# Masked products and states in wider vector instructions, and one subtraction issued a slot later, in a linear-attention pipeline

## What is computed

```python
qkv = x @ Wqkv.T + bqkv
q = (jax.nn.elu(q) + 1.0 + FEAT_EPS) / jnp.sqrt(E)
k = jax.nn.elu(k) + 1.0 + FEAT_EPS
kv_cumsum = jnp.cumsum(jnp.einsum('blhe,blhf->blhef', k, v), axis=1)
num = jnp.einsum('blhe,blhef->blhf', q, kv_cumsum)
den = jnp.einsum('blhe,blhe->blh', q, jnp.cumsum(k, axis=1))[..., None] + FEAT_EPS
out = (num / den).reshape(B, L, D)
```

## Time and profile before

| what | value |
|---|---|
| median of 3 runs | 722.83 us (722.69 to 724.22) |
| span of the profiled execution, first to last instruction | 705.1 us |
| its own total | the profile gives the span alone |
| busy PE, DVE, ACT, POOL | 629.5, 609.4, 494.0, 418.5 us |
| mean granted TensorE clock | 0.970 of full speed |
| first masked product, last masked product start | 31.0, 231.2 us |

### The profile page before, as it was taken

How to read it: one execution, slowest core, us unless ns; L and a number is a source line. 1 busy time by engine, 2 the same in 40 slices (tenths; PEclk the granted TensorE clock), 3 DMA queues, 4 the chain that set the end, 5 groups by cost and what they waited for, 6 DMA issues and landing times.

```text
span 705.1 us, 16639 instructions
## 1 busy us (share of the span) xinstructions
PE 629.5 (89%) x5448; PEld 323.9 (46%) x5448; DVE 609.4 (86%) x1566; ACT 494.0 (70%) x1007; POOL 418.5 (59%) x931
## 2 busy tenths in 40 slices
PE   4599689889887798899999999999999999899994
PEld 2366566666555322222323323233333322498994
DVE  6878999998977898899999999999999995686552
ACT  3634656766645347888888888888898889855662
POOL 6212666575656457135676787887777872566553
PEclk9899999999999959999999999999999999999997
DMA  6664133243263313016430120302103001456600
GB/s 180 176 215 122 49 111 108 97 158 106 92 203 98 89 46 110 26 54 202 121 91 2 58 69 13 113 25 87 39 19 109 25 12 35 138 171 175 173 31 12
DMA packets 42900, 66.26 MB, mean 94 GB/s; under 512 B 7948, under 2 KB 36335, under 8 KB 39808
## 3 DMA queue, kind: packets, MB, share of 16 engines
q1 hardware_dynamic: 39232, 56.73, 26.8%
q0 software_dynamic: 3296, 8.41, 3.3%
q10 hardware_dynamic: 288, 0.07, 0.0%
HBM read 41.64 MB, written 22.26 MB: 91 GB/s over the span
## 4 chain that ended last, share of the span: by engine, by line
PE 51%; DVE 20%; ACT 17%; issue 6%; POOL 3%; DMA 1%; SPq 1%; ACTq 0%; POOLq 0%; DVEq 0%
PE bank L1081 11%; ACT arena L2000 10%; PE pair L1070 7%; DVE arena L1569 6%; PE bank L1042 6%; PE pair L1331 4%; DVE arena L1402 4%; PE pair L1340 2%; PE bank L1340 2%; DVE arena L1431 2%; PE bank L1092 2%; PE bank L936 2%; ACT arena L1969 2%; PE bank L925 2%; DVE arena L1552 1%
## 5 line engine op out<-in xcount | busy, mean ns | idle before, releaser
L2000 ACT ACTIVATE arena<-pair 128x512 f32<-128x512 f32 x506 | 278.1, 602 | 50.5 <-PE pair L1070 48.6
L1569 DVE TENSOR_REDUCE arena<-bank 128x1 f32<-128x512 f32 x388 | 251.3, 682 | 7.5 <-PE bank L1042 6.5
L1070 PE MATMUL pair<-q_stack,k_stack 64*128 64x512 bf16 x506 | 158.0, 386 | 5.9 <-ACT arena L2000 5.3
L1042 PE MATMUL bank<-k_stack,q_stack 63*128 63x512 bf16 x388 | 137.4, 395 | 8.6 <-DVE arena L1569 4.8
L1081 PE MATMUL bank<-arena,values 128*9 128x512 f32 x1024 | 134.7, 598 | 1.6 <-ACT arena L2000 1.5
L1402 DVE TENSOR_TENSOR arena<-bank,cst 128x512 f32<-128x512 f32 x128 | 82.1, 682 | 15.6 <-PE bank L910 15.1
L1569 DVE TENSOR_REDUCE arena<-pair 128x1 f32<-128x512 f32 x124 | 84.3, 680 | 1.5 <-PE pair L1042 1.1
L1042 PEld LDWEIGHTS bank<-k_stack,q_stack 63*128 63x128 bf16 x388 | 33.3, 93 | 109.6 <-DVE arena L1569 24.9
L715 POOL TENSOR_TENSOR arena<-arena 128x32 f32<-128x32 f32 (+6 forms) x312 | 68.8, 220 | 24.4
L1070 PEld LDWEIGHTS pair<-q_stack,k_stack 64*128 64x128 bf16 x506 | 40.6, 93 | 48.6 <-ACT arena L2000 26.4
L1914 ACT ACTIVATE arena<-bank,den_eps 128x512 f32<-128x512 f32 x32 | 21.7, 677 | 41.2 <-PE bank L936 41.2
(11 more groups left out here) (301 smaller groups left out, 1262.0 us busy)
## 6 DMA issues: line engine op xcount, KB each, us to landing
softmax_parts<-arena SPq DMA_DIRECT2D x8, 768.0 KB
q_stack<-softmax_parts SPq DMA_DIRECT2D x48, 128.0 KB, 2.9
k_stack<-softmax_parts SPq DMA_DIRECT2D x48, 128.0 KB, 3.0
linear_parts<-arena SPq DMA_DIRECT2D x7, 768.0 KB, 3.7
q_stack<-linear_parts SPq DMA_DIRECT2D x42, 128.0 KB, 2.9
k_stack<-linear_parts SPq DMA_DIRECT2D x42, 128.0 KB, 2.9
arena<-in_L_ffn_w_dram SPq DMA_DIRECT2D x16, 256.0 KB, 4.5
v_all<-token_rows SPq DMA_DIRECT2D x20, 192.5 KB, 2.7
```

Of the source, the lines that this page charges most:

```text
L1042: pe.matmul(bank[:], qs[b % 2][rows, slot, qt * P:(qt + 1) * P], ks[b % 2][rows, slot, :], start=True, stop=True).then_inc(d_s_m, 1)
L1070: pe.matmul(score_bank(s)[:], ks[u][rows, 2 * g + x, kt * P:(kt + 1) * P], qs[u][rows, 2 * g + x, :], start=True, stop=True).then_inc(d_s_ ...
L1569: dve.reduce_max(mx[:, m % 2, col:col + 1], bank[:], AX).then_inc(d_s_mr, 1)
L2000: act.activation(pt[:, kt % 2, x, half, :], score_bank(s)[:], ACT.Exp, scale=SCALE).then_inc(d_s_e, 1)
```

## The change

Three edits on DVE, with the counts of the signals in the lists that wait for them. The two banks of the products become one PSUM tensor of 1,024 columns, `low`, with `bank[0]` and `bank[1]` as its halves, and `masked` takes them in one instruction with one signal. `state_masked` does three states in one instruction, by a pattern of four dimensions. `a_rest(s + 2, 0)` goes from slot 6 to slot 7, right before `a_rest(s + 2, 1)`.

```diff
@@ -83,7 +83,9 @@
-        k.bank = [top.enter_context(nc.psum_tensor(f"bank{i}", [P, 4 * P], F32)) for i in range(4)]
+        k.low = top.enter_context(nc.psum_tensor("low", [P, 8 * P], F32))
+        k.bank = [k.low[:, 0:512], k.low[:, 512:1024]]
+        k.bank += [top.enter_context(nc.psum_tensor(f"bank{i}", [P, 4 * P], F32)) for i in range(2, 4)]
         k.pair = [top.enter_context(nc.psum_tensor(f"pair{i}", [P, 8 * P], F32)) for i in range(2)]
@@ -902,7 +904,7 @@ products(g)
-                    wait(pe, s_am, 2 * g)
+                    wait(pe, s_am, g)
@@ -929,7 +931,7 @@ numerators(g)
-                    pe.wait_ge(s_am, 2 * g + 2)
+                    pe.wait_ge(s_am, g + 1)
@@ -1130,7 +1132,7 @@ early_maximum(m)
                     if m == 0:
-                        pe.wait_ge(s_am, 2 * B * NL)
+                        pe.wait_ge(s_am, B * NL)
@@ -1398,18 +1400,15 @@
                 def masked(g):
                     dve.wait_ge(s_at, g + 1)
                     wait(dve, s_nm, g - 1)
-                    for gg in range(2):
-                        dve.tensor_tensor(b_am[:, g % 2, gg], k.tiles(b_at[gg][:], GH), k.rep(k.causal, GH),
-                                          ALU.mult).then_inc(s_am, 1)
+                    dve.tensor_tensor(b_am[:, g % 2].rearrange("p u j q -> p (u j) q"), k.tiles(k.low[:], 2 * GH),
+                                      k.rep(k.causal, 2 * GH), ALU.mult).then_inc(s_am, 1)
 
                 def state_masked(b):
                     dve.wait_ge(s_sm, b + 1)
-                    w = H * (E + 1)
-                    for c in range(C - 1):
-                        last = dve.tensor_tensor(spad[b % 2][:, c, :].rearrange("p (h w) -> p h w", h=H)[:, :, 0:E + 1],
-                                                 b_z[:, c * w:(c + 1) * w].rearrange("p (h w) -> p h w", h=H),
-                                                 k.hmask.unsqueeze(2).to_broadcast([P, H, E + 1]), ALU.mult)
-                    last.then_inc(s_sp, 1)
+                    states = spad[b % 2].rearrange("p c (h w) -> p c h w", h=H)[:, :, :, 0:E + 1]
+                    sums = b_z[:, 0:(C - 1) * H * (E + 1)].rearrange("p (c h w) -> p c h w", c=C - 1, h=H)
+                    dve.tensor_tensor(states, sums, k.hmask.unsqueeze(1).unsqueeze(3).to_broadcast([P, C - 1, H, E + 1]),
+                                      ALU.mult).then_inc(s_sp, 1)
@@ -1794,8 +1793,8 @@
                             a_feature(s + 2, 1)
                             if s == -1:
                                 masked(0)
+                        if d == 7 and has(s + 2):
                             a_rest(s + 2, 0)
-                        if d == 7 and has(s + 2):
                             a_rest(s + 2, 1)
```

## The result

The changed kernel takes 729.33 us (median of 10 runs, 723.61 to 730.12), the kernel before, run beside it, 722.70 us (10 runs, 721.38 to 724.22). The ratio is 1.008, with a 95% interval of 1.0065 to 1.0095: 6.6 us slower where +1.6 was forecast, and above the range.

The account below looks back on a forecast made before the run. No single engine was named as bound; the chain of waits through the batch pipeline was costed alone. Terms 0.13 - 0.14 + 1.80 - 0.05 + 1.1 - 1.08 - 0.2 gave about +1.6 us, 724.4 us, range 721.0 to 726.8.

Parts of the forecast that it names:

- step 0 to 1: Pipeline transition without a stall to win: ScalarE's second part 1.80 us later, all on the chain; two masks save 0.14.
- Step 1 to 2: Pipeline transition: ScalarE 0.77 us late, but PE's next products wait for masked(1)'s end; nearly nothing, -0.05 us.
- Step 2 to 3: Pipeline transition: the port stall becomes a stall on ScalarE's queue, +0.37 us, likewise in the two transitions after it.
- The part behind step 5: Pipeline's end: masked(0) no longer waits for the stalled subtraction, -1.08 us; three merges on the chain, -0.2 us.
- what would show it: Trace signs: subtraction 0.68 us eight times, longer ScalarE wait, c_rest idle, masked(1) waiting over 2 us, DVE's busy time falling.
- The wide mask: Masked products on DVE: one instruction over 1,024 columns lasts 1.214 us and saves 0.067 us per pair.
- the 19 pieces: Pieces in a row on PE, without a gap, after its turn at 56.85 us; part of the chain delayed by 1.80 us.
- The time around the span: Part of the run outside the profiled span, taken as 17.7 us and left unchanged.
- A: The forecast, in the pipeline: ScalarE's wait replaces the port stall, 724.4 us; chance 0.47.
- B: Rival, at c_rest of slot 0: the next step does not wait for ScalarE, DVE's gain counts, -5.9, 717 us; chance 0.15.
- C: Rival, masked products: access over both banks costs another start, 1.9 us more than the forecast, 726.3 us; chance 0.15.
- D: Rival: each wide mask saves 0.15 us, or ScalarE's delay in s = 0 is partly taken up; 723.4 us; chance 0.23.

Follow-up runs that it names:

- e10: Changed kernel plus transposes nobody reads on PE, ahead of its real wait in slot 0 of steps 1 to 5; 710.73 us, ratio 1.0041 to before.
- e2: Kernel before with only the subtraction moved to slot 7, products and states masked as before; 714.6 us, ratio 1.0074.
- e7: Kernel before with only ScalarE's second part of q put behind the next slot's numerator copy, subtraction left in slot 6; 707.98 us, ratio 1.0002.
- e9: Changed kernel unaltered, timed on the third chip against the kernel before; 714.01 us, ratio 1.006.
- e1: Kernel before, no edit, run again to see its common profile; 708.85 us, ratio 1.0002.
- e6: Kernel before with the subtraction moved and ScalarE's second part of q behind the next numerator copy, without the merges; 704.59 us, ratio 0.9954.
- e3: Kernel before with only the two merges of masks, the subtraction left in its old slot; 708.2 us, ratio 0.9999.
- e4: Changed kernel with, from slot 7 of step 0 on, ScalarE's second part of q behind the next slot's numerator copy; 705.0 us, ratio 0.9955.

## Why the prediction was right or wrong

**The sum without the clock was right.** In e10, in steps with no star, against before: step 0 to 1 is 23.90 - 22.25 = +1.65 us, forecast 1.80 - 0.14 = +1.66. Step 1 to 2 is -0.19, forecast -0.05. Step 2 to 3 is +0.38, forecast +0.37; the changed kernel itself has +0.39, and +0.37 in step 4 to 5. The part behind step 5 is -1.27, though with a star, forecast -1.08 - 0.2. The signs of "what would show it" are in the trace, all but one: 0.68 us eight times, ScalarE's longer wait (1.96), c_rest's idle released by L1983, masked(1) waiting 2.73 us in s = 1, and no step shorter that was to be longer. The one is DVE's busy time, 8.6 us lower where 9 at least was forecast. The wide mask was forecast a little short, 1.214 for 1.224 us, since the time for a column was taken from two different kinds of instruction.

**The failed step is the one from 0 to 1**, and with it the -0.05 of step 1 to 2: "on which PE's turn, the products and masked(1) at 57.85 hang. +1.80, all on the chain". I shifted the 19 pieces behind PE's turn as a rigid block, with the durations of the trace of before. I worked out that the block would start late, but never that PE would stand idle longer for it, 2.80 instead of 0.80 us, and so never asked what the clock would do: the sum has no term for matmuls that run slower behind the wait, which is to say that it put them at nothing without a reason. The missing term, changed against before less the forecast: 3.11 - 1.66 = 1.45 us in step 0 to 1, 1.27 + 0.05 = 1.32 in step 1 to 2, 1.17 - 0.37 = 0.80 in step 3 to 4, 0.58 behind step 5, and 0.31 ahead of the first relu, which e2, e7, e9 and e10 have as well as the unaltered kernel of e1 (46.94) and which is no effect of the change. These are the remainders, step by step, of the 4.5 us between +6.05 and the forecast +1.57 at the row maximum, and not yet a price of the clock, as the execution shown of before is a fast one. Against e1, whose row maximum is at 236.99, that of e9 is 4.5 us later, and 2.9 are left above the forecast; between the medians 5.5 - 1.6 = 3.9 us are.

That the added idle brings on the added slow stretches is shown by e10, which took away a part of the idle in front of PE's turns and left ScalarE's order and the time of PE's turn as they were: 3.3 us of the 5.5 us of e9 went. That is the size of the missing term as far as it was measured; e10 leaves some of the idle and two slow stretches in place. What it leaves, 710.73 - 708.47 = 2.3 us, is near the forecast +1.6. The count of idle times above points the same way, six stretches behind six waits of 2.80 us and more, and none behind the 1.40 and 1.39 us that e10 leaves. So do single executions of e9: the mean granted clock was 0.967 to 0.968 in four of them, which took 708.9 to 711.2 us, and 0.956 to 0.962 in eight, at 713.8 to 715.4. The four are near the forecast, before's 708.47 + 1.6.

**The time around the span** was wrong too, but cancels: the sum was made on a difference.

**The rivals.** A was the mechanism, mis-sized by the clock. B stated rightly what DVE's gain is worth, and by what it is decided: with ScalarE's second part out of the way (e6), the steps with a stall are 26.59 - 25.53 = 1.06 us shorter each, for the stall's 1.09. C fell with e3. Of D, the merges shorten an undisturbed step by 0.10 us in e4 against e6 and by 0.24 in e3 against before, where I had counted one merge at 0.067; e3's time shows no gain clear of its interval.

**Still open.** Why an idle time of 1.5 to 2.1 us is followed by a slow stretch in one place and not in another, which makes the stretches of the kernel before (one in the shown execution, three in e1, partly at other places in e7), and so why one execution has a star where another of the same kernel has none. The executions of e9 at 709 us were not traced, so it is not shown that they lack the stretches behind the long waits. Whether a shorter filling would do, and whether filling the 2.1 us ahead of 223 us, which e10 left alone, would take away the last one, was not tried.

## What to carry to other kernels

When a wait moves from one engine to another, work out how long TensorE stands idle in the new order and not only when it starts again: here 2 us more idle cost 1.7 us by the delay and about 1.5 by slower matmuls behind it (step 0 to 1 of e9 against e10). An instruction moved later on one engine needs its reader moved on the other: the move alone lost 6 us, the order alone gave nothing, both together gained 3.3. Where the trace names an instruction that waits, look in the code for waits ahead of it that issue nothing.

## What was not expected of the hardware

- Behind PE's idle times of 2.80 and 2.91 us matmuls ran at the half clock, 1.2 GHz, from 0.7 and 1.3 us after the restart on, for some 3 us (L938 1.04 for 0.62 us, L976 1.06 for 0.60). Behind 0.80 us in the same places of the kernel before, and behind 1.40 us in e10, they did not. Behind idle times of 1.67 us both occurred in one trace: full speed behind the one that ended at 168.05 us, and behind the one at 139.88 an L1033 of 1.92 instead of 1.06 us, begun 1.8 us after it. The kernel before has such stretches too, behind 1.50 and 1.51 us of idle.
- Transposes whose result nobody reads, on an engine that would have stood idle, made the kernel 3.3 us faster.
- One vector instruction over two PSUM banks costs no second start: 1.224 us for 1,024 columns, against 0.681 for 512; but as neighbours begin before the end of the one in front, a step got 0.10 us shorter by all its merges together where ScalarE's second part was out of the way (e4 against e6), less than the 0.14 that the durations give for a single one; in e3 it was 0.24 us.
